# h2's columns by VectorE block transposition and a DRAM scratch instead of TensorE transposes

## The chip, the cores and the metric

The kernel runs on one core of a Trainium2 chip. The metric is device time in microseconds of one execution; 520.26 us is the median of three runs before the change. Engines: TensorE (PE), VectorE (DVE), ScalarE (ACT), GpSimd (POOL), and SyncE (SP), which issues most DMA transfers.

## The reference

The input x (16, 128, 64, 2) is a batch of complex weights; `h` is the real part of a state-space kernel table. Then come two residual layers on rows of length 1024, each behind a layernorm.

```python
K = einsum('chn,hnl->chl', Wc, exp(P)); h = K.real           # (16, 128, 1024)
h = h + einsum('bsk,nk->bsn', layernorm(h), weight * block_mask)
y = layernorm(h)
base = y @ W_base.T + b_base
weights = sparsemax(y @ W_router.T + b_router)               # 8 experts
h = h + base + einsum('bser,bse,ero->bso', y @ lora_A, weights, lora_B)
```

## The kernel before

The 2048 rows are cut into 16 tiles of 128 rows (16 batches by 8 heads). Before a loop, the weights are masked, centred and transposed and every fp32 operand is split into a high and a low part; a product is then three products (high by high, high by low, low by high). For each tile t:

- **Table.** `phases`, `exponentials`, `sines`, `v_factors`, `decay_b`, `table_v` and `table_b` build two small tables; `k_transposed` (PE, L439, sixteen matrix instructions) multiplies them, which gives the tile's columns in PSUM `turnp`. `k_high` (ACT, L717) and `k_low` (DVE, L1193) split them into `x1_hi` and `x1_lo`. `k_turn` (DVE, L1199) transposes 32 by 32 blocks of the same columns; SyncE writes them to a DRAM scratch `rows_out` in four pieces (L319) and reads them back as rows `h1` (L322).
- **First layer.** `attention` (PE, L455 on `acc_a`) multiplies; `k_sum` and `k_deviation` (ACT) with `h1_reciprocal` (DVE, L1204 to L1211) give the layernorm's factor; `attention_residual` (DVE, L1217) gives `h2`.
- **Second layer.** `h2_centre` and `h2_deviation` (ACT) centre h2 in place and take its deviation. `h2_transposes` (PE, L448) turns h2 into columns in `turnp`; `h2_high` (ACT, L752) and `h2_low` (DVE, L1246) split them. `lora_router` (L479, L481) and `base` (L455 on `acc_b`) multiply, `gates` (DVE, L1229 to L1240) forms the experts' weights, `gated_transpose`, `gated_high` and `gated_low` prepare them and `experts` multiplies. GpSimd's `add_bias` puts the mean back (L982) and adds the bias (L985); `result` (DVE, L1259) forms the output, which SyncE stores.

Each engine has its program written out by hand: a list of calls before the loop, then `step(t)`, run for tiles 2 to 11 in a loop of two steps a round and for 12 to 15 written out. Order across engines is by semaphores. A step on TensorE is: transposes of h2 of tile t-1, attention of t, table products of t+1, then lora_router, base and experts of t-1. `sines(t)` waits for `b_ready` of the tile before, since it overwrites factors that `table_b` reads.

## Time and profile before

| what | value |
|---|---|
| median of three runs | 520.26 us (519.95 to 521.26) |
| the profiled execution | 520.99 us, span 519.2 us |
| PE busy | 480.4 us (93%) |
| DVE busy | 408.4 us (79%) |
| ACT busy | 261.4 us (50%) |
| POOL busy | 125.7 us (24%) |

The span runs from the first to the last instruction of the profile; the execution's time has some 1.8 us more around it. Busy times of different engines overlap. Two operations of an engine can overlap by some 0.1 us at their borders, so that the time from one start to the next is what an operation costs its engine. Rows that name an idle time name the releaser behind an arrow.

### The profile page before, as it was taken

The page shows a single profiled execution, that of the slowest core. Times are in us where ns is not written, and L with a number is a line of the kernel's source. Part 1 is how long each engine was busy: PE and PEld are TensorE (multiplying, and loading weights), DVE is VectorE, ACT ScalarE, POOL GpSimd, SP SyncE. Part 2 cuts the span into 40 slices and gives each one's busy share as a digit, 9 for nine tenths or more (in the row PEclk, how much of TensorE's full clock was granted, in tenths as well). Part 3 has the DMA queues.
Part 4 walks back from the last instruction along what each step waited for, and adds up shares of the span by engine and source line. Part 5 has one row for each costly group of instructions (what it writes and reads, how often), then busy time and mean ns, then how long its engine had stood idle before and what let it go on. Part 6 is the DMA issues. An engine that isn't in the chain of part 4 may idle for free.

```text
span 519.2 us, 7441 instructions
## 1 busy us (share of the span) xinstructions
PE 480.4 (93%) x2467; PEld 406.1 (78%) x2467; DVE 408.4 (79%) x862; ACT 261.4 (50%) x476; POOL 125.7 (24%) x110
## 2 busy tenths in 40 slices
PE   1378789999999999999999999999999999999995
PEld 0267667877888888888888888888888888888884
DVE  7998979898988888888888888888888888854241
ACT  2848887576464626364554646362636455232200
POOL 0765597440303021020303030302102030303020
PEclk9998989999999999999999999999999999999999
DMA  8993113040403031212212030403121211313011
GB/s 286 391 338 51 63 42 122 1 127 6 126 3 110 16 88 38 81 45 68 59 40 86 10 116 0 109 17 88 38 81 47 67 56 26 96 31 92 1 40 40
DMA packets 28764, 40.83 MB, mean 79 GB/s; under 512 B 10760, under 2 KB 21192, under 8 KB 28744
## 3 DMA queue, kind: packets, MB, share of 16 engines
q1 hardware_dynamic: 28368, 40.49, 25.8%
q8 instruction: 10, 0.16, 0.1%
q10 hardware_dynamic: 376, 0.10, 0.1%
q14 instruction: 10, 0.08, 0.1%
HBM read 23.80 MB, written 16.78 MB: 78 GB/s over the span
## 4 chain that ended last, share of the span: by engine, by line
PE 90%; DVE 4%; issue 2%; ACT 2%; DMA 1%; POOL 1%; SPq 0%; DVEq 0%; POOLq 0%; ACTq 0%
PE acc_b L455 38%; PE acc_a L455 34%; PE turnp L439 6%; PE small L479 4%; PE turnp L448 3%; PE small L481 2%; PE acc_b L420 1%; PE acc_b L399 1%; DMA mask_raw<-in_L_attn_mask 1%; PE xps L429 1%; ACT wa_hi L668 1%; DVE mask_sum L1071 0%; DVE wa_raw L1080 0%; DVE wa_lo L1087 0%; PE small L487 0%
## 5 line engine op out<-in xcount | busy, mean ns | idle before, releaser
L982 POOL TENSOR_TENSOR h<-h,st 128x1024 f32<-128x1024 f32 x16 | 30.4, 1897 | 325.1 <-PE turnp L448 321.5
L455 PE MATMUL acc_a<-wa_hi,x_hi 128*128 128x512 f32 x256 | 83.2, 401 | 1.9 <-DVE wa_lo L1087 1.9
L455 PE MATMUL acc_b<-wb_hi,x_hi 128*128 128x512 f32 x256 | 83.9, 404 | 0.0
L455 PE MATMUL acc_a<-wa_hi,x_lo 128*128 128x512 f32 x256 | 81.3, 394 | 0.0
L455 PE MATMUL acc_a<-wa_lo,x_hi 128*128 128x512 f32 x256 | 81.2, 393 | 0.0
L455 PE MATMUL acc_b<-wb_lo,x_hi 128*128 128x512 f32 x256 | 80.5, 390 | 0.0
L455 PE MATMUL acc_b<-wb_hi,x_lo 128*128 128x512 f32 x256 | 80.5, 390 | 0.0
L455 PEld LDWEIGHTS acc_a<-wa_hi,x_lo 128*128 128x128 f32 x256 | 48.6, 190 | 10.4
L752 ACT ACTIVATE x_hi<-turnp 128x1024 fp32r<-128x1024 f32 x16 | 16.4, 1024 | 79.4 <-PE turnp L448 79.4
L455 PEld LDWEIGHTS acc_a<-wa_lo,x_hi 128*128 128x128 f32 x256 | 48.5, 189 | 10.0
L455 PEld LDWEIGHTS acc_b<-wb_hi,x_lo 128*128 128x128 f32 x256 | 48.1, 188 | 10.4
L455 PEld LDWEIGHTS acc_b<-wb_lo,x_hi 128*128 128x128 f32 x256 | 48.1, 188 | 10.4
L455 PEld LDWEIGHTS acc_a<-wa_hi,x_hi 128*128 128x128 f32 x256 | 47.3, 190 | 10.6 <-issue 2.0
L455 PEld LDWEIGHTS acc_b<-wb_hi,x_hi 128*128 128x128 f32 x256 | 44.8, 188 | 8.2
L1259 DVE SCALAR_TENSOR_TENSOR h<-acc_b,st,h 128x1024 f32<-128x1024 f32 (+1 forms) x17 | 20.7, 1221 | 25.5 <-PE acc_b L455 25.5
L985 POOL TENSOR_TENSOR h<-h,bias 128x1024 f32<-128x1024 f32 x16 | 39.5, 2467 | 1.3
L1193 DVE TENSOR_TENSOR x_lo<-turnp,x_hi 128x1024 fp32r<-128x1024 f32 x16 | 19.6, 1224 | 21.9 <-ACT x_hi L717 21.9
L439 PEld LDWEIGHTS turnp<-v_sb,b_sb 128*128 128x128 f32 x256 | 32.5, 200 | 3.6 <-issue 2.6
L439 PE MATMUL turnp<-v_sb,b_sb 128*128 128x128 f32 x256 | 32.9, 284 | 2.1 <-issue 2.1
L758 ACT ACTIVATE hw_hi<-small 128x128 fp32r<-128x128 f32 x16 | 4.4, 278 | 59.4 <-PE small L487 59.4
L479 PE MATMUL small<-wr,x_hi 128*128 128x272 f32 x128 | 32.2, 338 | 0.0
L692 ACT ACTIVATE er_t<-er_t 128x256 f32<-128x256 f32 x15 | 6.3, 419 | 48.9 <-DVE er_t L1112 48.9
(200 smaller groups left out, 937.0 us busy)
## 6 DMA issues: line engine op xcount, KB each, us to landing
h<-rows_out SPq DMA_DIRECT2D x16, 512.0 KB, 3.3
out<-h SPq DMA_DIRECT2D x15, 512.0 KB
rows_out<-b_sb SPq DMA_DIRECT2D x56, 128.0 KB, 2.3
mask_raw<-in_L_attn_mask SPq DMA_DIRECT2D x8, 512.0 KB, 9.9
wa_raw<-in_L_attn_weight SPq DMA_DIRECT2D x8, 512.0 KB, 10.5
wb_raw<-in_L_ffn_W_base SPq DMA_DIRECT2D x8, 512.0 KB, 6.7
rows_out<-tmp SPq DMA_DIRECT2D x8, 128.0 KB, 2.3
xn<-in_x SPq DMA_DIRECT2D x15, 64.0 KB
```

The costliest lines, as they stand in the source:

```text
L399: mm = pe.transpose(half_bank(i)[:, k * P:(k + 1) * P], every_eighth, ident)
L439: mm = pe.matmul(kt_pairs[:, h // HG, :, h % HG * C:(h % HG + 1) * C], b_sb[:, h, :, :].rearrange("p x y -> p (x y)"), v_sb[:, h, :, :], s ...
L448: mm = pe.transpose(turnp[:, k * P:(k + 1) * P], h2[par][:, k * P:(k + 1) * P], ident)
L455: return pe.matmul(cols, a, rows, start=first, stop=last)
L479: pe.matmul(small[:, 0:2 * CAT], x_hi[:, k, :], wr[:, k, :, :].rearrange("p s n -> p (s n)"), start=k == 0, stop=False)
L481: mm = pe.matmul(small[:, 0:CAT], x_lo[:, k, :], wr[:, k, 0, :], start=False, stop=k == KC - 1)
L692: act.activation(er_of(t), er_of(t), ACT.Exp).then_inc(tab_exp, 1)
L752: act.activation(x2_of(t)[0][:, :, :].rearrange("p k n -> p (k n)"), turnp[:, :], ACT.Copy)\
L982: pool.tensor_tensor(h2[par][:, :], h2[par][:, :], st2[:, par, 1:2].to_broadcast([P, L]), ALU.subtract)\
L985: pool.tensor_tensor(h2[par][:, :], h2[par][:, :], bias[:, :], ALU.add).then_inc(bias_added, 1)
L1193: dve.tensor_tensor(by_pair(lo), kt_pairs, by_pair(hi).bitcast(F), ALU.subtract).then_inc(kt_lo, 1)
L1259: dve.scalar_tensor_tensor(h, acc_b[:, cols], st2[:, par, 4:5], h, ALU.mult, ALU.add).then_inc(out_ready, 1)
```

## The change

In tiles 1 to 14 h2 doesn't go through TensorE. `h2_turn` (DVE) transposes 32 by 32 blocks of the centred h2 into `tmp`; `h2_columns` (SP) writes them to a DRAM scratch `cols_out` in four pieces and reads them back as columns into a buffer of their own, `x2_raw`; `h2_high` and `h2_low` split from there. Tiles 0 and 15 keep the transposes. ScalarE's `mean_add` puts the mean back, and GpSimd adds only the bias. `tmp` is now h2's, so `table_v` uses `turnp` for its second product, and `k_sum` and `k_deviation` write their unused output over `tmp` (`junk_tmp`). On VectorE `decay_b` moves out of `table_b`, `phases` to the start of a step. The orders before the loop are new on TensorE, ScalarE and VectorE; TensorE gets 14 products there (`keep_clock`) whose result nothing reads.

```diff
+        cols_out = nc.dram_tensor("cols_out", (4, 32, 4, KC * 32), F, kind="Internal").ap()
...
+        def by_dma(t):
+
+            return later(t, 1) and not at(t, TILES - 1)
+
+        def by_block(b):
+
+            return b[:, :, :].rearrange("p k (q r) -> p q k r", q=4)
+
+        x2_raw_block = x2_raw[:, :].rearrange("p (q k r) -> p q k r", q=4, k=KC)
...
+            def h2_columns(t):
+
+                sp.wait_ge(h2_turned, t)
+                for q in range(4):
+                    sp.dma_start(cols_out[:, :, q, :].rearrange("x i e -> i x e"),
+                                 tmp[q * 32:(q + 1) * 32, :].rearrange("i (x e) -> i x e", x=4)).then_inc(h2_out, 16)
+                sp.wait_ge(h2_out, t * 64)
+                sp.wait_ge(h2t_lo, t)
+                sp.dma_start(x2_raw[:, :], cols_out.rearrange("x i q e -> (x i) (q e)")).then_inc(h2_in, 16)
...
+                if by_dma(t):
+                    h2_columns(t)
...
+            def keep_clock(bank, n):
+
+                for _ in range(n):
+                    pe.matmul(bank, ident, kst[:, 0:2 * P], start=True, stop=True)
...
-                pe.wait_ge(kt_turned, t + 1)
-                h2_transposes(t - 1, 1 - par)
...
+            def mean_add(t, par):
+
+                if by_dma(t):
+                    act.wait_ge(h2_turned, t)
+                else:
+                    act.wait_ge(h2t_ready, 1 if at(t, 0) else 2)
+                act.wait_ge(h2_mean, t + 1)
+                mean = st2[:, par, 0:1]
+                act.activation(mean, mean, ACT.Copy, scale=1.0 / L).then_inc(mean_scaled, 1)
+                act.wait_ge(mean_scaled, t + 1)
+                act.wait_ge(h2_dev, t + 1)
+                act.activation(h2[par][:, :], h2[par][:, :], ACT.Identity, bias=mean).then_inc(mean_added, 1)
...
+                if later(t, 2):
+                    act.wait_ge(h2_out, t * 64 - 64)
+                act.activation(k_junk(t), h1[:, :], ACT.Copy, accum_out=st1[:, 0:1]).then_inc(h1_summed, 1)
 
...
-                act.wait_ge(h2t_ready, t + 1)
-                act.activation(x2_of(t)[0][:, :, :].rearrange("p k n -> p (k n)"), turnp[:, :], ACT.Copy)\
-                    .then_inc(h2t_hi, 1)
+                if by_dma(t):
+                    act.wait_ge(h2_in, t * 16)
+                    act.wait_ge(ffn_ready, t)
+                else:
+                    act.wait_ge(h2t_ready, 1 if at(t, 0) else 2)
+                hi = x2_of(t)[0]
+                if by_dma(t):
+                    act.activation(by_block(hi), x2_raw_block, ACT.Copy).then_inc(h2t_hi, 1)
+                else:
+                    act.activation(hi[:, :, :].rearrange("p k n -> p (k n)"), turnp[:, :], ACT.Copy).then_inc(h2t_hi, 1)
...
-                act.wait_ge(ffn_ready, t - 1)
-                h2_high(t - 1)
                 k_sum(t)
                 k_deviation(t)
+                h2_high(t - 1)
+                mean_add(t - 1, 1 - par)
                 if real(t + 2):
                     x_rows_twice(t + 2)
-                    exp_and_sin(t + 2)
+                    exponentials(t + 2)
+                    sines(t + 2)
...
-                pool.wait_ge(h2t_ready, t + 1)
-                pool.wait_ge(h2_dev, t + 1)
-                pool.tensor_tensor(h2[par][:, :], h2[par][:, :], st2[:, par, 1:2].to_broadcast([P, L]), ALU.subtract)\
-                    .then_inc(mean_added, 1)
...
-                second = v_second if not later(t, 2) else tmp[:, :].rearrange("p (h a c) -> p h a c", h=HT, a=NA)
+                second = v_second
...
-                decay_b(t)
                 dve.wait_ge(h1_in, t * 16)
+                dve.wait_ge(h2_out, t * 64 - 128)
+                dve.wait_ge(h1_dev, t)
...
+            def h2_turn(t, par):
+
+                dve.wait_ge(h2_dev, t + 1)
+                if at(t, 1):
+                    dve.wait_ge(h1_in, 32)
+                dve.transpose(tmp[:, :].rearrange("p (x k r) -> p k x r", x=4, k=KC), h2[par][:, :]).then_inc(h2_turned, 1)
...
-                dve.tensor_tensor(s[:, 4:5], s[:, 5:6], s[:, 7:8], ALU.mult).then_inc(s_chain, 1)
+                dve.tensor_scalar(s[:, 4:5], s[:, 5:6], s[:, 7:8], None, ALU.mult).then_inc(s_chain, 1)
...
-                dve.tensor_tensor(lo[:, :, :].rearrange("p k n -> p (k n)"), turnp[:, :],
-                                  hi[:, :, :].bitcast(F).rearrange("p k n -> p (k n)"), ALU.subtract)\
-                    .then_inc(h2t_lo, 1)
+                if by_dma(t):
+                    dve.tensor_tensor(by_block(lo), x2_raw_block, by_block(hi).bitcast(F), ALU.subtract).then_inc(h2t_lo, 1)
+                else:
+                    dve.tensor_tensor(lo[:, :, :].rearrange("p k n -> p (k n)"), turnp[:, :],
+                                      hi[:, :, :].bitcast(F).rearrange("p k n -> p (k n)"), ALU.subtract)\
+                        .then_inc(h2t_lo, 1)
...
+                if real(t + 2):
+                    phases(t + 2)
                 h2_low(t - 1)
-                h2_reciprocal(t - 1, 1 - par)
                 if real(t + 1):
                     table_b(t + 1)
                 h1_reciprocal(t)
-                if real(t + 2):
-                    phases(t + 2)
+                h2_reciprocal(t - 1, 1 - par)
                 dve.wait_ge(out_stored[par], t * 8 - 8 * par)
                 attention_residual(t, par)
+                if real(t + 2):
+                    v_factors(t + 2)
+                    decay_b(t + 2)
                 if real(t + 1):
                     k_low(t + 1)
+                    k_turn(t + 1)
                 gates(t - 1, 1 - par)
-                if real(t + 1):
-                    k_turn(t + 1)
-                if real(t + 2):
-                    v_factors(t + 2)
+                if by_dma(t):
+                    h2_turn(t, par)
                 gated_low(t - 1)
...
+            k_turn(2)
             k_low(2)
+            h2_turn(1, 1)
+            v_factors(3)
             gated_low(0)
```

TensorE at a step's border, before: the last products of `experts`, h2's transposes, and the first attention products.

```order
L455 MATMUL acc_b<-lb_hi,hw_hi 128x512
L455 MATMUL acc_b<-lb_lo,hw_hi 128x512 x2
L455 MATMUL acc_b<-lb_hi,hw_lo 128x512 x2
L448 MATMUL turnp<-kst,h_0 128x128 [waits h2_centred,kt_turned]
L448 MATMUL turnp<-kst,h_0 128x128 x7
L455 MATMUL acc_a<-wa_hi,x_hi 128x512 [waits kt_lo]
L455 MATMUL acc_a<-wa_hi,x_hi 128x512
L455 MATMUL acc_a<-wa_lo,x_hi 128x512 x2
```

The same border after the change (here L492 is the product helper):

```order
L492 MATMUL acc_b<-lb_hi,hw_hi 128x512
L492 MATMUL acc_b<-lb_lo,hw_hi 128x512 x2
L492 MATMUL acc_b<-lb_hi,hw_lo 128x512 x2
L492 MATMUL acc_a<-wa_hi,x_hi 128x512 [waits kt_lo]
L492 MATMUL acc_a<-wa_hi,x_hi 128x512
L492 MATMUL acc_a<-wa_lo,x_hi 128x512 x2
L492 MATMUL acc_a<-wa_hi,x_lo 128x512 x2
```

The eight transposes and their waits for `h2_centred` and `kt_turned` are gone; attention's own wait for `kt_lo` is left.

ScalarE across a step's border, before: `gated_high`, `h2_high` (L752), then `k_sum` and `k_deviation`.

```order
L758 ACTIVATE hw_hi<-small 128x128 [waits hwt_ready]
L752 ACTIVATE x_hi<-turnp 128x1024 [waits h2t_ready,ffn_ready]
L738 REGISTER_ALU [waits h1_in]
L739 ACTIVATE junk,st<-h 128x1024 [waits rs1_chain]
L743 ACTIVATE st<-st 128x1 [waits h1_summed]
L744 ISA
L745 ACTIVATE junk,st<-h,st 128x1024 [waits h1_stat]
L746 REGISTER_ALU
L747 ACTIVATE st<-st,kst 128x1 [waits h1_stat]
```

And after: `h2_high` is L819 and the first operation of `mean_add` L785.

```order
L826 ACTIVATE hw_hi<-small 128x128 [waits hwt_ready]
L797 REGISTER_ALU [waits h1_in]
L799 ISA [waits rs1_chain]
L800 ACTIVATE junk_tmp,st<-h 128x1024 [waits h2_out]
L804 ACTIVATE st<-st 128x1 [waits h1_summed]
L805 ISA
L806 ACTIVATE junk_tmp,st<-h,st 128x1024 [waits h1_stat]
L807 REGISTER_ALU
L808 ACTIVATE st<-st,kst 128x1 [waits h1_stat]
L813 REGISTER_ALU
L819 ACTIVATE x_hi<-x_raw 128x4x8x32 [waits ffn_ready,h2_in]
L785 ACTIVATE st<-st 128x1 [waits h2_mean,h2_turned]
```

`h2_high` moved behind `k_sum` and `k_deviation`, reads `x2_raw`, and waits for the scratch's read (`h2_in`); `k_sum` waits for the scratch's writes (`h2_out`).

VectorE at a step's end, before: `gated_low`, `table_v` (L1164 to L1167), `result` (L1259), and then the next step's `h2_low` (L1246).

```order
L1253 TENSOR_TENSOR hw_lo<-small,hw_hi 128x128 [waits hwt_hi]
L1163 REGISTER_ALU [waits b_ready,kt_ready,w_ready]
L1164 TENSOR_TENSOR v_sb<-xps,u 128x1024 [waits v_chain]
L1165 TENSOR_TENSOR tmp<-xps,u 128x1024
L1166 REGISTER_ALU
L1167 TENSOR_TENSOR v_sb<-tmp,v_sb 128x1024 [waits v_chain]
L1259 SCALAR_TENSOR_TENSOR h_1<-acc_b,st,h_1 128x1024 [waits bias_added,ffn_ready]
L1246 TENSOR_TENSOR x_lo<-turnp,x_hi 128x1024 [waits h2t_hi]
L1204 TENSOR_SCALAR st<-st 128x1 [waits h2_dev]
```

And after, from the last operation of `gates` (L1316) on: L1268 is `h2_turn`, L1231 to L1234 `table_v`, L1338 `result`.

```order
L1316 TENSOR_TENSOR hw_sb<-cat,gs 128x128 [waits gate_chain]
L1268 STREAM_TRANSPOSE tmp<-h_0 128x8x4x32 [waits h2_dev]
L1332 TENSOR_TENSOR hw_lo<-small,hw_hi 128x128 [waits hwt_hi]
L1230 REGISTER_ALU [waits b_ready,kt_turned,kt_ready,w_ready]
L1231 TENSOR_TENSOR v_sb<-xps,u 128x1024 [waits v_chain]
L1232 TENSOR_TENSOR turnp<-xps,u 128x1024
L1233 REGISTER_ALU
L1234 TENSOR_TENSOR v_sb<-turnp,v_sb 128x1024 [waits v_chain]
L1338 SCALAR_TENSOR_TENSOR h_1<-acc_b,st,h_1 128x1024 [waits bias_added,ffn_ready]
```

`h2_turn` stands between `gates` and `gated_low`, and `table_v` writes `turnp` where it wrote `tmp`.

## Rows read from the trace of the kernel before

**Rows 1.** Page, part 4: shares of the span on the chain that ended last.

```profile
PE 90%; DVE 4%; issue 2%; ACT 2%; DMA 1%; POOL 1%; SPq 0%; DVEq 0%; POOLq 0%; ACTq 0%
```

**Rows 2.** Chain in order of time, two loop steps (start us, us, what).

```profile
219.02 0.87 PE turnp L448 x8
219.89 10.92 PE acc_a L455 x48
230.81 1.78 PE turnp L439 x16
...
247.15 0.87 PE turnp L448 x8
...
472.83 10.93 PE acc_a L455 x48
```

**Rows 3.** Busy time by stretch (us), engine by engine, clock, DMA, GB/s.

```profile
27.80:104.83 77.03, 66.04 (x355) 55.99 (x354) 68.21 (x121) 56.13 (x102) 48.72 (x45) 0.96 0.33 96
190.88:219.02 28.14, 28.14 (x148) 23.89 (x146) 23.34 (x49) 14.29 (x26) 4.29 (x2) 1.00 0.20 58
```

**Rows 4.** VectorE, one loop step (start us, us, what, idle before).

```profile
222.87 1.49 DVE L1211 TENSOR_TENSOR st<-st 128x1 f32<-128x1 f32 x1
...
224.94 1.23 DVE L1183 TENSOR_TENSOR b_sb<-pp,qq 128x1024 f32<-128x1024 f32 x1
...
228.48 0.15 DVE L1204 TENSOR_SCALAR st<-st 128x1 f32<-128x1 f32 x1
...
229.23 0.16 DVE L1211 TENSOR_TENSOR st<-st 128x1 f32<-128x1 f32 x1
229.35 0.42 DVE L1112 TENSOR_TENSOR er_t<-dec,mul 128x256 f32<-128x256 f32 x1
...
231.74 1.28 DVE L1217 SCALAR_TENSOR_TENSOR h<-acc_a,st,h 128x1024 f32<-128x1024 f32 x1
...
234.73 1.23 DVE L1193 TENSOR_TENSOR x_lo<-turnp,x_hi 128x1024 fp32r<-128x1024 f32 x1 [1.70 <-ACT x_hi L717]
235.87 0.29 DVE L1229 COPY cat<-small 128x136 f32<-128x136 f32 x1
...
238.63 2.12 DVE L1199 STREAM_TRANSPOSE b_sb<-turnp 128x1024 f32<-128x1024 f32 x1
240.59 0.27 DVE L1137 TENSOR_TENSOR xy<-xy,er_t 128x128 f32<-128x128 f32 x1
```

**Rows 5.** SyncE's queue, one loop step (start us, us, what).

```profile
240.77 1.76 SPq L319 DMA_DIRECT2D rows_out<-b_sb  x4
244.37 0.34 SPq L322 DMA_DIRECT2D h<-rows_out  x1
```

**Rows 6.** Line L322, the read of the scratch: issue to landing.

```profile
DMA to landing us min/median/max: 3.2/3.3/4.1
```

**Rows 7.** ScalarE, one loop step (start us, us, what, idle before).

```profile
219.93 1.03 ACT L752 ACTIVATE x_hi<-turnp 128x1024 fp32r<-128x1024 f32 x1 [6.07 <-PE turnp L448]
...
230.25 1.28 ACT L700 ACT_TABLE_LOAD   x1
231.86 0.35 ACT L700 ACTIVATE xy<-gh_t,kst 128x64 f32<-128x64 f32 x1 [0.32 <-DVE a_t L1123]
...
233.31 0.48 ACT L705 ACTIVATE qq<-gh_t,kst 128x128 f32<-128x128 f32 x1
```

**Rows 8.** VectorE before the loop (start us, us, what).

```profile
81.03 0.28 DVE L1174 TENSOR_TENSOR pp<-pp,er_t 128x128 f32<-128x128 f32 x1
...
81.56 0.29 DVE L1137 TENSOR_TENSOR xy<-xy,er_t 128x128 f32<-128x128 f32 x1
...
82.69 1.22 DVE L1246 TENSOR_TENSOR x_lo<-turnp,x_hi 128x1024 fp32r<-128x1024 f32 x1
83.83 1.22 DVE L1164 TENSOR_TENSOR v_sb<-xps,u 128x1024 f32<-128x1024 f32 x1
```

**Rows 9.** GpSimd, the same loop step.

```profile
221.95 2.40 POOL L985 TENSOR_TENSOR h<-h,bias 128x1024 f32<-128x1024 f32 x1
```

More of the change, by code:

```diff
@@ L123, in build_vit_tower @@
         b_sb = sb("b_sb", [P, HT, NB1, NB0])
+        with nc.sbuf_tensor("junk_tmp", [P, L], BF) as junk_tmp:
+            pass
         tmp = sb("tmp", [P, L])
@@ L126, in build_vit_tower @@
         x1_raw, x1_lo = sb_twice("x1_raw", [P, L], F, "x1_lo", [P, KC, P])
-        x2_hi, x2_lo = sb("x2_hi", [P, KC, P], FR), sb("x2_lo", [P, KC, P], FR)
+        x2_hi = sb("x2_hi", [P, KC, P], FR)
+        x2_lo = sb("x2_lo", [P, KC, P], FR)
+        with nc.sbuf_tensor("junk", [P, L], BF) as junk:
+            pass
+        x2_raw = sb("x2_raw", [P, L])
         h1 = sb("h1", [P, L])
         h2 = [sb(f"h2_{i}", [P, L]) for i in range(2)]
-        junk = sb("junk", [P, L], BF)
         hw_sb = sb("hw_sb", [P, E, R])
@@ L591, in _ @@
             attention(1, 1)
-            attention(1, 2)
             wb_half(10)
@@ L596, in _ @@
             h2_transposes(0, 0)
+            attention(1, 2)
             wb_half(12)
@@ L608, in _ @@
             lora_router(0)
-            k_transposed(2)
+            x_transposes(3)
+            attention(1, 7)
             pe.wait_ge(wb_high, 2 * NWT)
@@ L813, in _ @@
             wa_highs(13)
-            q_tanh(1)
+            k_sum(0)
             wa_highs(14)
             wa_highs(15)
+            k_deviation(0)
             wb_highs(0)
+            wb_highs(1)
+            q_sines(1)
             x_rows_twice(2)
-            wb_highs(1)
+            k_high(1)
+            sines(2)
+            wb_highs(2)
+            exponentials(2)
+            wb_highs(3)
+            wb_highs(4)
+            h2_centre(0, 0)
+            wb_highs(5)
+            wb_highs(6)
+            h2_deviation(0, 0)
+            wb_highs(7)
+            wb_highs(8)
+            wb_highs(9)
+            wb_highs(10)
+            wb_highs(11)
+            wb_highs(12)
             act.wait_ge(lora_in, 16 * KC)
@@ L822, in _ @@
             act.activation(wr[:, :, 0, :], cat_raw, ACT.Copy).then_inc(cat_hi, 1)
-            k_sum(0)
-            k_deviation(0)
-            q_sines(1)
-            wb_highs(2)
-            wb_highs(3)
-            k_high(1)
-            wb_highs(4)
-            wb_highs(5)
-            exponentials(2)
-            wb_highs(6)
-            wb_highs(7)
-            sines(2)
-            wb_highs(8)
-            wb_highs(9)
-            h2_centre(0, 0)
-            wb_highs(10)
-            wb_highs(11)
-            wb_highs(12)
             wb_highs(13)
+            h2_high(0)
             x_rows_twice(3)
-            h2_high(0)
-            h2_deviation(0, 0)
+            k_sum(1)
             wb_highs(14)
             wb_highs(15)
-            k_sum(1)
+            mean_add(0, 0)
             k_deviation(1)
             h2_centre(1, 1)
+            k_high(2)
+            sines(3)
             act.wait_ge(lorb_in, 16)
             act.activation(lb_hi[:, :], lb_raw[:, :], ACT.Copy).then_inc(lorb_hi, 1)
-            k_high(2)
+            h2_deviation(1, 1)
+            gated_high(0)
             exponentials(3)
-            gated_high(0)
-            sines(3)
-            h2_deviation(1, 1)
             steps(act, step)
@@ L861, in _ @@
             h2_high(TILES - 1)
+            mean_add(TILES - 1, 1)
             gated_high(TILES - 1)
@@ L1308, in _ @@
             wa_mask(1)
-            reciprocal_of_norm(0)
+            wa_mask(2)
+            v_factors(0)
+            wa_lows(0)
+            wa_mask(3)
+            wa_lows(1)
+            decay_b(0)
             mask_sums(4)
-            wa_mask(2)
-            wa_mask(3)
+            table_v(0)
+            mask_sums(5)
             wa_mask(4)
-            decay_b(0)
-            v_factors(0)
-            mask_sums(5)
-            wa_lows(0)
-            wa_lows(1)
-            table_v(0)
+            wa_lows(4)
             mask_sums(6)
-            wa_lows(4)
+            phases(1)
             wa_lows(5)
+            wa_mask(5)
+            q_arguments(1)
             mask_sums(7)
-            wa_mask(5)
-            phases(1)
             k_low(0)
-            wa_mask(6)
+            k_turn(0)
             wa_lows(8)
             wa_lows(9)
-            q_arguments(1)
+            wa_mask(6)
             wa_mask(7)
+            router_columns()
             decay_b(1)
-            k_turn(0)
+            reciprocal_of_tanh(1)
             wa_lows(12)
@@ L1353, in _ @@
             wb_lows(6)
+            k_turn(1)
             wb_lows(7)
-            k_turn(1)
             wb_lows(8)
+            decay_b(2)
             wb_lows(9)
@@ L1360, in _ @@
             wb_lows(11)
+            v_factors(2)
             wb_lows(12)
             wb_lows(13)
-            decay_b(2)
-            v_factors(2)
             h2_low(0)
@@ L1368, in _ @@
             wb_lows(15)
-            phases(3)
-            h2_reciprocal(0, 0)
             h1_reciprocal(1)
@@ L1373, in _ @@
             attention_residual(1, 1)
+            phases(3)
+            h2_reciprocal(0, 0)
             dve.wait_ge(biasr_in, 16)
             gates(0, 0)
+            k_turn(2)
             k_low(2)
+            h2_turn(1, 1)
+            v_factors(3)
             gated_low(0)
-            k_turn(2)
-            v_factors(3)
+            decay_b(3)
+            table_v(3)
             dve.wait_ge(ffn_ready, 1)
             result(0, 0)
-            table_v(3)
             steps(dve, step)
```

108 lines of the change are left out of this document (60 added, 48 removed).

## The prediction

> **What bounds the kernel now.** I read the chain that ended last first: 90% of it is TensorE [rows 1]. Then the same chain in order of time, over the loop [rows 2]: eight transposes of h2 (0.87 us), 48 attention products (10.92), the table products (1.78), and so on to the next transposes at 247.15. No piece of another engine stands between them, so a step lasts 247.15 - 219.02 = 28.13 us and the loop is TensorE without a gap; from 219.89 to 472.83 nine steps average 28.10. The reader is to see in the busy times by stretch (second row of [rows 3]) that the next engine, VectorE, does 23.3 us of that step and that the clock is full (1.00, the 2.4 GHz level). Before the loop it is otherwise: from 27.8 to 104.8 us TensorE is busy 66.0 of 77.0 us and VectorE 68.2 (first row of [rows 3]); there nobody binds alone.
>
> **The change part by part.** *Removed:* the eight transposes of each step whose h2 goes by DMA. In the loop that is 0.87 us of TensorE [rows 2], so TensorE alone would need 28.13 - 0.87 = 27.26. From the attention products of tile 3 to those of tile 15 there are twelve such steps, all of which the change touches; the most to be had there is 12 x (28.10 - 27.26) = 10.1 us. The last tile keeps its transposes, so the tail gives nothing.
>
> *Added:* the columns must now make a round trip, and what counts is when the round trip, started by one step's h2_turn, lets the next step's h2_turn start. I sum it from the end of h2_turn.
>
> The scratch. k_turn does the same journey today: it ends at 238.63 + 2.12 = 240.75 [rows 4], its four writes are issued at 240.77 and the read at 244.37 [rows 5], 3.62 us after; the read lands 3.3 us after issue in the median [rows 6]. Sizes and row lengths of h2's four writes and one read are the same, so 6.92. SyncE is free for it: k_turn stands a gates block and a transposition ahead of h2_turn, 2.76 plus over 1 us, against the 3.62 + 0.34 that its own sequence takes [rows 4, 5]; nearly even, so at worst some tenths. Behind the read waits only the store of the tile before.
>
> ScalarE. h2_high is 1.03 [rows 7]; with two handovers of 0.02 (240.75 to 240.77) the sum is 7.99. k_sum and k_deviation stand ahead of it, but wait only for the writes, not the read, so I cost them nothing; their cover is the 3.3 us read. mean_add comes behind h2_high, and with it, one small and one full-width operation later, GpSimd's bias addition starts.
>
> VectorE. h2_low: 1.14 (82.69 to 83.83) [rows 8]. table_b without its decay: 3.54 (224.94 to 228.48) [rows 4]. Sum 12.67. VectorE is not late for h2_low: gated_low, table_v, result and phases need about 7.3 us of the 8.
>
> GpSimd. The bias addition takes 2.40 [rows 9]. Today it meets one small VectorE operation with both inputs in SBUF: L1211 takes 1.49 there and 0.16 six us later [rows 4], and its end, 224.36, is the end of GpSimd's 2.40 (224.35). After the change the addition falls beside h2_low and table_b. Nothing here shows it beside those, so the bounds are 0 and 2.40; I take 2.40, since L1211 stood still until the whole addition was done: 15.07 at b_ready. The Trainium skill (SBUF — State Buffer, "Who interferes with whom") says that a VectorE instruction with two SBUF inputs blocks fully against a GpSimd one that reads SBUF, and h2_low, which read PSUM, becomes such a one; by that rule the cost is 2.40 and speaks against the change, by the 0.16 of an undisturbed operation it would be nothing and the sum 2.40 shorter.
>
> ScalarE again: the sines wait for b_ready with their table load in front, which today is early. Load 1.28, the six sines 1.93 (231.86 to 233.31 + 0.48) [rows 7]: 18.28. The stretch of h1's and h2's reciprocals and the residual lies beside that (0.87 + 0.87 + 1.28 = 3.0) [rows 4].
>
> VectorE to the next h2_turn: decay_b 0.53, v_factors 1.13 [rows 8], k_low 1.14, k_turn 1.96, gates 2.76 [rows 4]: 7.52, sum 25.80.
>
> h2_turn itself. The only transposition shown takes 2.12 for 1024 columns; every other operation of that width takes 1.2 [rows 4]. k_turn writes with a step of eight values; h2_turn reads SBUF straight through and writes runs of 32. Bounds 1.2 and 2.12; since its access is that of the plain operations, I take 1.22. The Trainium skill (Vector Engine (DVE) Microarchitecture Reference, 3.8 "The reshape front-end and per-opcode configuration") has the transposing array at one element per cycle per lane; the 2.12 of k_turn doesn't agree with it as it stands, and no run here shows whether the write step is why. By the rule the round trip is 27.0, by the row 27.9.
>
> The round trip is thus 27.02 us, against TensorE's 27.26. Two cycles that close, with a read that lands between 3.2 and 4.1 [rows 6], don't run at the longer one exactly: I take 27.4 for a step, where TensorE waits a tenth or two at the table products. Twelve steps: 12 x (28.10 - 27.4) = 8.4.
>
> VectorE's own load: 23.34 busy, less 1.33 for L1211 (now a one-input form that need not stand still), plus 1.22 and at most 2.40, is 25.6; it stays below 27.26, by less than before.
>
> *Moved:* the orders before the loop. TensorE idles 77.0 - 66.0 = 11.0 us there and VectorE 8.8 [rows 3]. The new order does k_turn(0) some 2 us earlier against VectorE's other work, and fills TensorE's pauses with 14 products that keep it active (its granted clock is 0.96 there); against that, gated_low(0) now stands behind h2_turn(1) and v_factors(3), so the first experts can wait, and the first scratch trip starts only there. I bound this by a loss of 3 and a gain of 6, and take a gain of 1.5, a fifth of what VectorE idles.
>
> Sum: the profiled execution took 520.99 (span 519.2); less 8.4 and 1.5 is 511.1. The median shown is 520.26, 0.73 below the profiled one, so 510.4. About 0.3% (1.6 us) is what a measurement here can tell from no change.
>
> **Rivals.** *The transposition costs 2.12.* For: the only row of its kind. Against: the write step. The round trip is then 27.92, with the same tenth or two 28.05, no better than today's 28.10: 12 x 0.05 + 1.5 leaves 518.2, on the edge of no change. TensorE would simply wait for b_ready instead of transposing.
>
> *The scratch trip is longer than k_turn's (slower).* Its writes follow the read of h1, and its read runs up against the store of the tile before; both are 512 KB. Each us beyond 6.92 prolongs each of twelve steps once the 0.24 of slack is gone; from 8.0 on the kernel is slower by the loop. With landings at the 4.1 shown as the longest, for writes (2.3 now) and read alike, the trip is 6.92 + 1.8 + 0.8 = 9.5; halfway, 8.2, a step is 28.3 and with half the prologue's gain lost the time is 520.3 + 2.4 - 0.8 = 522; at 9.5 it is 29.6, 520.3 + 18 - 0.8 = 538. Against: in the loop the median lies 0.1 above the shortest.
>
> *The cover holds better.* GpSimd finds no gap until table_b is through; then the sum is 24.6, steps are TensorE's 27.26, and with an order before the loop that gains 4 the time is 520.3 - 10.1 - 4 = 506.
>
> **How the numbers follow.** Forecast case (steps of 27.3 to 27.6; 507 to 514): 0.50. Transposition dear (518): 0.20. Longer trip (522 to 538): 0.12. Better cover (506): 0.18. Range: 504 (a full 10.1 and the bound of 6 before the loop) to 520.5 (the dear transposition without any gain before the loop); that leaves out the longer trip and little else. Faster by over 0.3% (below 518.7): 0.50 + 0.18 + 0.12 of the dear transposition's 0.20 = 0.80; within 0.3%: the other 0.08; slower 0.12.
>
> **What would show it.** In the profile after: h2's transposes gone from the chain but for two tiles; a step of 27.3 to 27.6; x2_raw landing about 6.9 us after h2_turn's end; h2_turn at 1.2 or 2.1; one of h2_low and table_b's operations at 3.6 instead of 1.2, ending with GpSimd's addition; TensorE's only wait in a step at the table products for b_ready. Wrong would be a step above 28, or a wait at lora_router, which would say that h2_low, not table_b, is late.

## The result, and the profile after

The changed kernel takes 539.12 us (median of 4 runs, 536.75 to 540.3), the kernel before 520.47 on the same chip: a ratio of 1.0351, 95% interval 1.0309 to 1.0393. It is slower by 18.7 us where 10 were forecast as a gain, 28.7 off the predicted 510.4 and outside the range.

The profiled execution took 538.15 us (span 536.3). The chain that ended last, by engine, against 90% TensorE before [rows 1]:

```profile
DVE 28%; DMA 20%; ACT 15%; PE 14%; SPq 13%; issue 8%; DVEq 1%; ACTq 0%
```

The chain is no longer one engine; it is a round trip through VectorE, SyncE, the DMA engines and ScalarE. The same chain in order of time over two steps, its pieces of 0.8 us and more, from the landing of the first writes to the next table (start us, us, what). L368 writes h2's columns to the scratch and L372 reads them back, L819 is h2_high, L1251 to L1254 are table_b, L742 the load of the sines' table, L1261 k_low, L1275 k_turn, L800 k_sum:

```profile
251.90 3.13 DMA cols_out<-tmp
255.05 3.22 DMA x_raw<-cols_out
258.29 1.07 ACT x_hi L819
259.71 0.82 issue
260.53 1.22 DVE b_sb L1251
261.75 3.36 DVE tmp L1252
265.13 1.24 DVE b_sb L1254
266.44 1.28 ACT L742
271.53 1.14 DVE x_lo L1261
272.67 2.15 DVE b_sb L1275
276.15 2.36 DMA rows_out<-b_sb
278.53 3.73 DMA h<-rows_out
282.43 1.28 ACT L800
283.72 1.16 ACT junk_tmp L800 x2
...
290.12 1.22 DVE b_sb L1251
...
318.62 1.22 DVE b_sb L1251
```

Where TensorE alone stood in [rows 2], there is none of it in these two steps. Table_b starts at 260.53, 290.12, 318.62: steps of 29.59 and 28.50 in turn, against 28.13. The alternation has two chains: one step goes through the columns' trip, the next through h1's read and ScalarE. Busy times by stretch, answering to [rows 3]; the second row is two steps:

```profile
27.80:104.83 77.03, 66.02 (x369) 54.97 (x369) 66.13 (x131) 58.28 (x109) 44.90 (x43) 0.98 0.35 101
250.20:308.20 58.00, 55.93 (x275) 45.93 (x274) 50.94 (x102) 33.83 (x58) 6.62 (x2) 1.00 0.31 93
```

TensorE pauses 2.07 us in two steps at full clock, and VectorE has 7 us to spare: neither binds alone. SyncE's queue in those two steps, answering to [rows 5] (L338 writes k_turn's result, L341 reads h1):

```profile
246.39 1.76 SPq L338 DMA_DIRECT2D rows_out<-b_sb  x4
250.08 0.34 SPq L341 DMA_DIRECT2D h<-rows_out  x1
250.54 1.88 SPq L368 DMA_DIRECT2D cols_out<-tmp  x4
255.05 0.34 SPq L372 DMA_DIRECT2D x_raw<-cols_out  x1
...
278.53 0.34 SPq L341 DMA_DIRECT2D h<-rows_out  x1
278.98 1.99 SPq L368 DMA_DIRECT2D cols_out<-tmp  x4
283.70 0.34 SPq L372 DMA_DIRECT2D x_raw<-cols_out  x1
```

The columns' first write is issued 0.46 us after h1's read, each time. From there to the scratch's read passes 4.51 and 4.72 us; for k_turn's result, in the kernel before, it was 3.60 (240.77 to 244.37). The read itself lands 3.2 us after issue in the median, as [rows 6] would have it. VectorE from h2_low (L1323) to h2_turn (L1268), and GpSimd's addition, answering to [rows 4, 9]:

```profile
259.39 1.22 DVE L1323 TENSOR_TENSOR x_lo<-x_raw,x_hi 128x1024 fp32r<-128x1024 f32 x1 [0.76 <-ACT x_hi L819]
260.53 1.22 DVE L1251 TENSOR_TENSOR b_sb<-pp,qq 128x1024 f32<-128x1024 f32 x1
261.67 3.43 DVE L1252 TENSOR_TENSOR tmp<-pp,qq 128x1024 f32<-128x1024 f32 x1
265.13 1.23 DVE L1254 TENSOR_TENSOR b_sb<-b_sb,tmp 128x1024 f32<-128x1024 f32 x1
...
277.40 1.24 DVE L1268 STREAM_TRANSPOSE tmp<-h 128x1024 f32<-128x1024 f32 x1
```

```profile
260.71 3.30 POOL L1052 TENSOR_TENSOR h<-h,bias 128x1024 f32<-128x1024 f32 x1 [25.10 <-ACT h L788]
```

L1252 takes 3.43 us instead of 1.22 and ends 1.1 after GpSimd's 264.01: it stood still until the addition was done. GpSimd's took 3.30 instead of 2.40, its first 0.9 to 1.0 beside L1251. The transposition h2_turn is 1.24. Last, ScalarE in the second of the two steps, against [rows 7]:

```profile
282.43 1.28 ACT L800 ACT_TABLE_LOAD   x1 [4.24 <-DMA h<-rows_out]
283.72 1.06 ACT L800 ACTIVATE junk_tmp<-h 128x1024 bf16<-128x1024 f32 x1
...
286.40 1.28 ACT L808 ACT_TABLE_LOAD   x1
287.70 0.29 ACT L808 ACTIVATE st<-st,kst 128x1 f32<-128x1 f32 x1
287.90 1.04 ACT L819 ACTIVATE x_hi<-x_raw 128x1024 fp32r<-128x1024 f32 x1
```

Two loads of a function table, in the first step of each loop round alone. ScalarE enters the loop with the table of the exponentials, but comes back to its top with that of the roots, so the loads stand at the top for both; k1_sqrt below bears that out. In the step before, k_sum starts with the writes' landing (255.06) and h2_high at 258.29, 3.24 after the read's issue; here it is 4.20. The first of the two loads ends when the writes land (283.71) and costs nothing; the second prolongs the trip.

### The profile page after: what moved, and what is told of

Read it like the earlier page. It is cut to its first block, busy times and chain, and to the rows that moved or that the text cites. A ratio compares the mean times of both kernels' runs of the same rounds, so it can differ in the third digit from the quotient of the medians.

```text
span 536.3 us, 7446 instructions
## 1 busy us (share of the span) xinstructions
PE 480.0 (89%) x2379; PEld 397.3 (74%) x2379; DVE 432.2 (81%) x876; ACT 293.3 (55%) x516; POOL 106.0 (20%) x94
## 4 chain that ended last, share of the span: by engine, by line
DVE 28%; DMA 20%; ACT 15%; PE 14%; SPq 13%; issue 8%; DVEq 1%; ACTq 0%
DVE tmp L1252 8%; PE acc_b L492 7%; DMA cols_out<-tmp 6%; DMA rows_out<-b_sb 6%; DVE b_sb L1275 5%; DMA x_raw<-cols_out 5%; PE acc_a L492 4%; DMA h<-rows_out 3%; SPq L352 3%; SPq L338 3%; DVE b_sb L1254 3%; DVE b_sb L1251 3%; ACT L742 3%; ACT x_hi L819 2%; DVE x_lo L1261 2%
## 5 line engine op out<-in xcount | busy, mean ns | idle before, releaser
L1052 POOL TENSOR_TENSOR h<-h,bias 128x1024 f32<-128x1024 f32 x16 | 50.2, 3139 | 365.2 <-ACT h L788 365.2
L492 PE MATMUL acc_b<-wb_hi,x_hi 128*128 128x512 f32 x256 | 84.3, 405 | 0.0
L492 PE MATMUL acc_a<-wa_hi,x_hi 128*128 128x512 f32 x256 | 82.7, 399 | 0.8 <-ACT wa_hi L710 0.8
L492 PE MATMUL acc_a<-wa_lo,x_hi 128*128 128x512 f32 x256 | 81.5, 395 | 0.0
L492 PE MATMUL acc_b<-wb_lo,x_hi 128*128 128x512 f32 x256 | 81.1, 393 | 0.0
L492 PE MATMUL acc_a<-wa_hi,x_lo 128*128 128x512 f32 x256 | 80.9, 392 | 0.0
L492 PE MATMUL acc_b<-wb_hi,x_lo 128*128 128x512 f32 x256 | 80.9, 392 | 0.0
L492 PEld LDWEIGHTS acc_a<-wa_hi,x_lo 128*128 128x128 f32 x256 | 48.3, 189 | 11.0
L492 PEld LDWEIGHTS acc_a<-wa_lo,x_hi 128*128 128x128 f32 x256 | 48.5, 189 | 10.5
L492 PEld LDWEIGHTS acc_b<-wb_hi,x_lo 128*128 128x128 f32 x256 | 48.1, 188 | 10.9
L492 PEld LDWEIGHTS acc_b<-wb_lo,x_hi 128*128 128x128 f32 x256 | 48.1, 188 | 10.7
L492 PEld LDWEIGHTS acc_a<-wa_hi,x_hi 128*128 128x128 f32 x256 | 48.0, 189 | 10.7 <-issue 1.0
L476 PE MATMUL turnp<-v_sb,b_sb 128*128 128x128 f32 x256 | 34.8, 293 | 20.1 <-issue 11.0
L476 PEld LDWEIGHTS turnp<-v_sb,b_sb 128*128 128x128 f32 x256 | 32.5, 205 | 25.7 <-issue 25.5
L492 PEld LDWEIGHTS acc_b<-wb_hi,x_hi 128*128 128x128 f32 x256 | 45.5, 191 | 7.3
L1252 DVE TENSOR_TENSOR tmp<-pp,qq 128x1024 f32<-128x1024 f32 x13 | 44.6, 3432 | 0.0
L800 ACT ACTIVATE junk_tmp<-h 128x1024 bf16<-128x1024 f32 x14 | 14.8, 1058 | 51.1 <-DMA cols_out<-tmp 51.0
L1338 DVE SCALAR_TENSOR_TENSOR h<-acc_b,st,h 128x1024 f32<-128x1024 f32 (+1 forms) x17 | 20.7, 1220 | 24.1 <-PE acc_b L492 24.1
L1323 DVE TENSOR_TENSOR x_lo<-x_raw,x_hi 128x1024 fp32r<-128x1024 f32 x14 | 17.2, 1225 | 24.7 <-ACT x_hi L819 24.7
```

The costliest lines, as they stand in the source:

```text
L476: mm = pe.matmul(kt_pairs[:, h // HG, :, h % HG * C:(h % HG + 1) * C], b_sb[:, h, :, :].rearrange("p x y -> p (x y)"), v_sb[:, h, :, :], s ...
L492: return pe.matmul(cols, a, rows, start=first, stop=last)
L1052: pool.tensor_tensor(h2[par][:, :], h2[par][:, :], bias[:, :], ALU.add).then_inc(bias_added, 1)
L1252: dve.tensor_tensor(b_terms(tmp), *b_factors(t, 1), ALU.mult).then_inc(b_chain, 2)
L1323: dve.tensor_tensor(by_block(lo), x2_raw_block, by_block(hi).bitcast(F), ALU.subtract).then_inc(h2t_lo, 1)
L1338: dve.scalar_tensor_tensor(h, acc_b[:, cols], st2[:, par, 4:5], h, ALU.mult, ALU.add).then_inc(out_ready, 1)
```

## The experiments

A step is the time from one tile's first attention product to the next one's; attention(3) and attention(15) are where it starts for these tiles. k4 and k8 leave out part or all of h1's read and k9 the reordering of k_turn's result in every second step, so these three are for timing alone. In the diffs `...` marks what is left out.

| kernel | median us | ratio to before, 95% interval | attention(3) | step | attention(15) |
|---|---|---|---|---|---|
| before | 520.06 to 520.54 | | 135.25 | 28.13 | 472.59 |
| after | 539.12 | 1.035 [1.031, 1.039] | 139.01 | 29.6 / 28.6 | 489.55 |
| k1_sqrt | 537.06 | 1.030 [1.027, 1.033] | 140.62 | 28.7 to 29.2 | 489.86 |
| k2_bias_late | 513.65 | 0.987 [0.984, 0.989] | 136.84 | 27.42 | 465.61 |
| k4_h1_quarter | 524.64 | 1.008 [1.006, 1.011] | 139.49 | 28.7 / 27.7 | 475.81 |
| k5_orders_alone | 527.50 | 1.013 [1.010, 1.015] | 138.91 | 28.31 | 478.55 |
| k8_no_h1_read | 519.48 | 0.998 [0.997, 1.000] | 139.67 | 27.4 to 27.6 | 471.13 |
| k9_plain_turn | 537.98 | 1.035 [1.033, 1.037] | 139.88 | 27.6 to 31.2 | 488.44 |
| k7_shift64 | 523.03 | 1.005 [1.004, 1.007] | 135.08 | 28.31 | 474.51 |
| k10_bias_late_aligned | 517.82 | 0.996 [0.995, 0.998] | 135.75 | 27.72 | 468.23 |
| k12_bias_late_placed | 510.27 | 0.982 [0.980, 0.983] | 135.29 | 27.23 | 461.75 |
| k14_up128 | 527.70 | 1.014 [1.013, 1.016] | 134.45 | 28.62 | 477.64 |
| k15_up256 | 520.46 | 1.000 [0.999, 1.001] | 134.90 | 28.13 | 472.24 |
| k16_all_up128 | 519.91 | 0.999 [0.998, 1.000] | 133.93 | 28.13 | 471.28 |
| k13_all | 509.20 | 0.980 [0.978, 0.982] | 134.43 | 27.23 | 460.90 |

The column of steps leaves out a few of the twelve at either end: 27.83 and 31.84 in the changed kernel, 27.96, 30.33, 31.59 and 28.05 in k1, 28.51 in k8.

**k1_sqrt**

```diff
             exponentials(3)
+            act.activation(wa_neg[:, 0:1], col(COL_HALF), ACT.Sqrt)
             steps(act, step)
```

> One Sqrt of a single column is added on ScalarE after exponentials(3), so that the loop is entered with the same function table as its back edge has, and the two table loads at the loop's top go. Theory A (the loop step is the round trip h2_turn - scratch - h2_high - table_b - sines - next h2_turn, and every microsecond on it counts): the first step of each loop round falls from 29.6 to about 28.4 us, five rounds, so 539.1 - 6 = about 533 us. Rival B (the scratch trip alone is late, ScalarE's loads lie beside it): steps still alternate 28.4 and 29.6, 539 us.

The loads went and so did the alternation, but the time fell by 2.1, not 6, and the runs of the two kernels overlap (534.94 to 538.52 against 536.75 to 540.3). In the eight steps from 164 to 366 us the trip from h2_turn's end to h2_high is 8.3 to 8.8 us, where the changed kernel has 8.1 to 8.3 and 9.2 to 9.35 in turn. From the read's issue to h2_high it is 3.3 in all of them instead of 4.2 in every second one, so ScalarE no longer outlasts the read. But from the first write's issue to the read's it is 4.90 instead of 4.74, and the 3.3 is 3.32 where the changed kernel's steps without loads have 3.21. So the loads did prolong every second step, as A has it, and part of what they cost came back in the transfers; why those became longer is open. What the loads are worth in the whole time is not shown by this run.

**k2_bias_late**

```diff
             def add_bias(t, par):
+                if real(t + 2):
+                    pool.wait_ge(b_ready, t + 3)
                 pool.wait_ge(mean_added, t + 1)
```

> GpSimd's addition of the bias waits until table_b is through, so it no longer stands beside table_b on VectorE. Theory A: L1252's operation falls from 3.43 to 1.22 us and each of 12 steps with it by about 2.2, unless TensorE's 27.26 or a later wait comes first: steps of 27.3 to 27.6, about 516 to 521 us. Rival B (the scratch trip sets the step whatever stands behind it on VectorE, since the trip's start would be moved too, or the addition meets another operation on the path instead): less than 0.5 per step, 533 to 539 us.

Faster than expected: 25.5 us off the changed kernel, with trips as long as there (8.2 to 9.7). Of the 23.9 us that attention(15) comes sooner, 2.2 lie ahead of attention(3). Table_b's second operation (L1254 here) is back at 1.22, and GpSimd's addition at 2.4:

```profile
251.90 1.22 DVE L1253 TENSOR_TENSOR b_sb<-pp,qq 128x1024 f32<-128x1024 f32 x1
253.03 1.22 DVE L1254 TENSOR_TENSOR tmp<-pp,qq 128x1024 f32<-128x1024 f32 x1
```

```profile
255.67 2.40 POOL L1054 TENSOR_TENSOR h<-h,bias 128x1024 f32<-128x1024 f32 x1 [24.48 <-DVE b_sb L1256]
```

The steps are all TensorE's again: in its chain, the products of the experts run straight into the next tile's attention:

```profile
213.75 5.51 PE acc_b L492 x24
219.26 10.99 PE acc_a L492 x48
230.25 1.78 PE turnp L476 x16
...
246.67 10.99 PE acc_a L492 x48
```

247.15 - 219.02 is now 246.67 - 219.26 = 27.41. Taking 2.2 us out of steps of 29.6 and 28.5 leaves 27.4 and 26.3, both within it. Rival B falls: the trip sets the step only together with what stands behind it. But TensorE itself needs 27.42, not the 27.26 of the prediction, 10.99 us for 48 products instead of 10.93; k7 follows that up.

**k4_h1_quarter**

```diff
-                sp.dma_start(h1[:, :], rows_out.rearrange("g r l -> (g r) l")).then_inc(h1_in, 16)
+                if later(t, 2):
+                    sp.dma_start(h1[0:32, :], rows_out[0]).then_inc(h1_in, 16)
...
```

> From the third tile on only a quarter of h1 (128 KB of 512) is read back from its scratch; three quarters of h1 keep the values of an earlier tile. Theory A with contention (the writes of h2's columns land late because h1's read was issued 0.4 us ahead of them): the writes land about 2.3 us after issue instead of 3.1 to 3.4, the trip falls from 8.07 to about 7.0 us, a step by 1.1, and the time to about 525 us; the steps that wait for h1 at the loop's top gain too. Rival C (the writes are late by themselves, 2.3 was never theirs): trip 8.0 as before, 536 to 539 us.

As A expected (524.64 against 525). Page, the DMA issues, in the changed kernel and then in this one (KB each, median us from issue to landing):

```profile
cols_out<-tmp SPq DMA_DIRECT2D x56, 128.0 KB, 3.4
```

```profile
cols_out<-tmp SPq DMA_DIRECT2D x56, 128.0 KB, 2.4
```

The same 128 KB writes land 1.0 us sooner when h1's read ahead of them is a quarter; the read of the scratch stays (3.3 instead of 3.2). From the first write's issue to the scratch's read it is 3.79 to 3.85 in eleven steps. The trip is 7.2 to 7.7 us, and 8.3 in the steps with ScalarE's loads. The Trainium skill (SBUF — State Buffer, "Can I just issue two DMAs to hit both halves?") says that all DMAs of a kernel share the same 16 engines and largely serialize; at the 358 GB/s that the summary of that page gives for transfers between HBM and SBUF, the 384 KB left out are an estimated 1.1 us. The 1.0 measured agrees with it.

**k5_orders_alone** (the last columns through TensorE as before; new orders kept)

```diff
         def by_dma(t):
 
-            return later(t, 1) and not at(t, TILES - 1)
+            return False
...
             def step(t, par):
+                pe.wait_ge(kt_turned, t + 1)
+                if real(t + 1):
+                    pe.wait_ge(v_ready, t + 2)
+                h2_transposes(t - 1, 1 - par)
                 pe.wait_ge(kt_lo, t + 1)
...
```

> All of h2's columns go by TensorE again; the new orders and the mean on ScalarE stay. Theory A (the round trip makes the loop slow): steps go back to TensorE's 28.1 us, and with the earlier start of the loop's work (some 4 us before the loop) the time is 515 to 521 us. Rival D (the new orders themselves, or GpSimd's addition beside table_b, cost the time): 528 us or more, with steps above 28.5.

527.5: neither fits. The loop is TensorE's without a gap, as A says, but at 28.31 instead of 28.13 (2.2 us in twelve steps; k7 below has the same 28.31), and attention(3) starts at 138.91, 3.7 later than before. So the new orders had no gain before the loop to give this kernel, though in the changed kernel the residual of the second tile starts at 89.8 us instead of 94.2. Its added wait for v_ready, which the kernel before doesn't have at that place, is part of this start, so the 3.7 isn't the orders' alone.

**k8_no_h1_read** (with k1's Sqrt besides)

```diff
+                if later(t, 3):
+                    sp.dma_start(h1[0:N, 0:2], lam).then_inc(h1_in, 16)
+                    return
                 sp.wait_ge(k_out, (t + 1) * 16 * Q)
...
             exponentials(3)
+            act.activation(wa_neg[:, 0:1], col(COL_HALF), ACT.Sqrt)
...
                 dve.wait_ge(h2_out, t * 64 - 128)
+                dve.wait_ge(k_out, t * 16 * Q)
                 dve.wait_ge(h1_dev, t)
```

> From the fourth tile on the read of h1 is left out (h1 keeps old values; a read of a few bytes stands in its place, and SyncE doesn't wait for the rows before it issues the columns' writes); the Sqrt of k1_sqrt is in. GpSimd's addition still stands beside table_b. Theory A' (the predicted sum was right but for the scratch trip; measured in the changed kernel, what follows the trip takes 20.3 us, and the trip is long by h1's read, SyncE's order and ScalarE's two table loads): the trip falls from 8.2 to 9.3 to about 6.9 to 7.2 us, a step to 27.4 to 27.6, so the time to 539.1 - 12 x 1.7 = about 519 us (the loss before the loop stays). Rival (what follows the trip is long as well, or the trip is long by itself): steps of 28 us or more, 526 us or more.

519.48 against 519. The trip is 6.8 to 7.2 us in eleven steps, the prediction's 6.92, and the step 27.4 to 27.6, its 27.4, with GpSimd's block still in table_b (in most steps 3.31 at its third operation instead of its second). One trip, from h2_turn's end (245.28) by the first write, the scratch's read and h2_high, and TensorE's chain beside it:

```profile
244.04 1.24 DVE L1273 STREAM_TRANSPOSE tmp<-h 128x1024 f32<-128x1024 f32 x1
245.30 1.75 SPq L371 DMA_DIRECT2D cols_out<-tmp  x4
248.98 0.34 SPq L375 DMA_DIRECT2D x_raw<-cols_out  x1
252.36 1.06 ACT L822 ACTIVATE x_hi<-x_raw 128x1024 fp32r<-128x1024 f32 x1 [0.38 <-DMA x_raw<-cols_out]
...
250.01 10.99 PE acc_a L495 x48
```

This is the run that names the failed step: with the trip as long as the prediction had it, the loop no longer waits for the round trip. From 140 to 415 us its chain is TensorE's alone, which needs 27.42 at these addresses (k2). So the step of 27.4 doesn't confirm the other terms of the sum; those are measured in the changed kernel.

**k9_plain_turn**

```diff
...
+                elif par == 0:
+                    dve.transpose(turned_of(t), turnp[:, :]).then_inc(kt_turned, 1)
...
```

> In every second step of the loop k_turn writes its result straight through instead of with a step of eight values (h1 is then wrong in those steps); in the other steps it is as it was. Theory W (the write step, not the transposition, makes k_turn 2.2 us): the straight ones take 1.24 us, as h2_turn does, the others 2.2, and the loop gains about 1 us in every second step, some 5 to 6 us in all: 533 us. Rival P (the read from PSUM makes it 2.2): all stay at 2.2, 539 us.

W holds for the operation. Duration in ns, min/median/max, of k_turn written straight (L1278) and with the step (L1280):

```profile
L1278 DVE STREAM_TRANSPOSE b_sb<-turnp x7: 1239/1240/1240, 126.9 to 476.4; 128x1024 f32<-128x1024 f32 x7
L1280 DVE STREAM_TRANSPOSE b_sb<-turnp x6: 2195/2220/2233, 156.9 to 447.4; 128x1024 f32<-128x1024 f32 x6
```

Both read the same PSUM, so PSUM isn't it. The Trainium skill (SBUF — State Buffer, "Door 1: The DMA port swizzle") says that an access that goes on to another 16-byte line of SBUF pays for it; a step of eight values does so each time, and 2.22 against 1.24 agrees. For the time, the expectation fell: 1.1 us less instead of 5 to 6, which the spread of the runs doesn't tell from nothing. In several of these steps table_b ended 9.3 to 9.8 us after h2_high's start instead of 8.1, with GpSimd's block at its first operation; that wasn't followed further.

**k7_shift64**

```diff
-        gt, neg_gt, flip = sb("gt", [P, 1]), sb("neg_gt", [P, 1]), sb("flip", [P, 1])
+        signs_sb = sb("signs_sb", [P, 3])
+        gt, neg_gt, flip = (signs_sb[:, i:i + 1] for i in range(3))
```

> The kernel before, with its three one-value columns gt, neg_gt and flip laid into one buffer of three, as in the changed kernel; that moves every later SBUF buffer, x1 and x2 among them, down by 64 bytes and changes nothing else. Theory L (TensorE's products took 10.99 us for 48 instead of 10.93, and a step 27.42 instead of 27.26, because x1 and x2 lie 64 bytes off): a step of 28.3 us instead of 28.13, about 522.5 us. Rival (the new orders or the other engines' accesses slow the products): 28.13, 520.5 us.

Theory L: 523.03. The kernel before, with nothing but later buffers 64 bytes lower, has the slower products:

```profile
220.24 11.00 PE acc_a L456 x48
```

**k10_bias_late_aligned** (k2 with this besides)

```diff
-        dt_k, dt_r, dt_p, dt_w = (sb(n, [P, 2]) for n in ("dt_k", "dt_r", "dt_p", "dt_w"))
+        dt_sb, dt_w = sb("dt_sb", [P, 6]), sb("dt_w", [P, 2])
+        dt_k, dt_r, dt_p = (dt_sb[:, 2 * i:2 * i + 2] for i in range(3))
```

> k2_bias_late with three small buffers merged as well, so that x1, x2 and all else behind them lie 64 bytes lower still, at a multiple of 128 bytes as in the kernel before. Theory L: 48 products at 10.93 us, a step of 27.26 instead of 27.42, 513.65 - 12 x 0.16 - about 0.5 = 511.3 us. Rival: 10.99 and 513.6 us as without.

Both fall: slower than k2, 517.82, 48 products at 11.15 to 11.16 and steps of 27.72. A multiple of 128 bytes isn't what helps; at 128 bytes off the products are worse than at 64.

**k12_bias_late_placed** (k2 with this besides)

```diff
-        signs_sb = sb("signs_sb", [P, 3])
-        gt, neg_gt, flip = (signs_sb[:, i:i + 1] for i in range(3))
+        signs_sb = sb("signs_sb", [P, 24])
+        gt, neg_gt, flip, tau = (signs_sb[:, i:i + 1] for i in range(4))
+        wa_sum = signs_sb[:, 8:8 + NWT]
...
```

> k2_bias_late with the buffers from xn on laid 64 bytes higher (the one buffer of three columns takes 96 bytes, and tau and wa_sum lie in it), so that v, b, tmp, x1 and x2 have the addresses of the kernel before. Theory L' (the products' rate goes with these addresses: 10.93 us for 48 there, 11.00 at 64 bytes less, 11.16 at 128 less): 10.93 again, a step of 27.26, which is the figure that the prediction had for TensorE alone; 513.65 - 12 x 0.16 - 0.5 = about 511.2 us. Rival (something else of these kernels slows the products by 0.6%): 11.0 and 513.6.

L' holds: 510.27 and a step of 27.23, with the products no slower than in the kernel before:

```profile
217.15 10.88 PE acc_a L493 x48
```

**k14_up128, k15_up256, k16_all_up128** (the kernel before with 128 or 256 bytes left free ahead of xn; or 128 ahead of every buffer, the weights' too; the diff is k14's)

```diff
+        sb("pad", [P, 32])
         xn = sb("xn", [P, N, 2])
```

> The kernel before with 128 bytes left free ahead of xn, so that everything behind lies 128 bytes higher. Theory L1 (the rate falls with each step down and goes on rising upward): 48 products in under 10.93 us, a step below 28.1, 517 to 520 us. Theory L2 (the equal offset of x1, x2 and of the weights' buffers is the best there is): 11.0 to 11.2, 523 to 527 us.

> The same with 256 bytes left free. By L1 faster still or as with 128, by L2 slower than before: 523 to 528 us; if the pattern repeats within 256 bytes it is the time of the kernel before, 520.3 us.

> The kernel before with 128 bytes left free ahead of all its buffers, so that the weights' buffers lie 128 bytes higher as well as x1 and x2 (in k14_up128 x1, x2 alone moved, and 48 products took 11.15 to 11.19 us). Theory R (what counts is how x1 and x2, VectorE's and ScalarE's buffers lie against the weights' buffers): 10.93 us and 520.4. Theory M (what counts is the address itself, modulo 256): 11.16 us and 527.7.

Attention's 48 products in the three, in this order:

```profile
220.52 11.19 PE acc_a L456 x48
```

```profile
219.54 10.92 PE acc_a L456 x48
```

```profile
218.58 10.92 PE acc_a L456 x48
```

L2 holds (527.7, just above its range), with a pattern that repeats within 256 bytes, and R: moving the weights' buffers along brings the rate back. Which of the buffers that moved together has to lie so, x1 and x2 or those that VectorE and ScalarE use, is not shown.

**k13_all** (k12 with k1's Sqrt and SyncE's load of x moved)

```diff
             k_rows(2)
-            load_x(4)
...
             h2_columns(1)
+            load_x(4)
```

> k12_bias_late_placed with the Sqrt of k1_sqrt, so that the two table loads leave the loop's top and the first trip, and with SyncE's load of tile 4's x moved behind the first trip's read, so that the first writes of h2's columns don't stand behind it. In the trace of k12 that load (0.62 us) is on the chain ahead of the first trip, and the table loads in it (1.0). Theory A (the loop is TensorE's, 27.23 a step, only the first trip is to be had): 510.3 - 1.6 = 508.7 us. Rival (something else before the loop is late in its place): 510.3.

509.2, the fastest, 2.0% below the kernel before. The first trip fell from 11.05 us in k12 to 10.0 and attention(3) came 0.9 sooner; A's 1.6 was a little too much. The runs of the two overlap (509.56 to 512.07 and 508.97 to 511.17), so of the 1.1 between the medians only these 0.9 in the traces are shown.

## Why the prediction was wrong

The round trip was the right model, and its sum failed above all in one term. The trace of the changed kernel over one step, from h2_turn's end (250.20) to the next (278.64), by the prediction's terms:

| term | predicted | measured |
|---|---|---|
| scratch trip, h2_turn's end to h2_high | 6.92 | 8.09; 9.26 in the next step; 8.77 mean of ten |
| h2_high, h2_low, table_b with GpSimd's block | 8.15 | 8.07 |
| sines to h2_turn's end | 11.95 | 12.28 |
| sum | 27.02 | 28.44; next step 29.56 |

The third term is 0.33 over as well, in pieces of a tenth or less in and between its operations (k_turn costs 2.05 for 1.96). With the last two terms as measured, the predicted trip would give 27.27, so the 0.24 of slack against TensorE's 27.26 was never there.

- **The step that failed** is "Sizes and row lengths of h2's four writes and one read are the same, so 6.92. SyncE is free for it". The mean excess of 1.85 has three parts. The writes: about 1.1, since h1's read is issued 0.46 us ahead of them and k_turn's own writes had no such neighbour; k4 shows 1.0 of it. SyncE: 0.3, since the first write waits behind h1's read in its queue; the prediction called it "nearly even, so at worst some tenths", but of a margin of 0.24 that alone was too much. ScalarE: 1.0 in every second step, because "so I cost them nothing; their cover is the 3.3 us read" holds only without the two table loads; k1, without them, still has a mean trip of 8.55. In k8, without these, the trip is 7.0 and the loop TensorE's.
- **What it had as the rival.** The longer trip, with 28.3 us a step at 8.2 and 29.6 at 9.5, is what happened: 28.4 at 8.1 and 29.6 at 9.3. Its chance of 0.12 was too low: the prediction itself named h1's 512 KB read as the neighbour, and set it aside by landings in a trace where the two never met.
- **GpSimd's block** was right: 2.40 taken, 2.21 measured (3.43 - 1.22). The Trainium skill (SBUF — State Buffer, "Who interferes with whom") says that a VectorE instruction with two SBUF inputs contends with a GpSimd one that reads SBUF; the trace agrees. That the term was right doesn't make the block harmless: with the trip as it is, moving the addition behind table_b (k2) gives the loop back to TensorE. The prediction had this as better cover at 506; k12 measures 510.27, and 27.23 a step against its 27.26, without the 4 us before the loop. That 510.27 is nearly the forecast's 510.4 is luck: the forecast had slower steps of 27.4 and a gain of 1.5 before the loop.
- **h2_turn** was right: 1.24 against 1.22; the rival of 2.12 fell, and k9 shows why.
- **What lies before the loop** was wrong: a gain of 1.5 taken, a loss of 3.8 measured at attention(3) (139.01 against 135.25). In this trace the loss is not ahead of tile 2, whose attention starts at 105.32 against 105.67; it is in the step from there to tile 3, the one with the first trip, which lasts 33.69 instead of 29.58. In k1, k2, k4 and k8 tile 2 starts at 106.7 to 108.3, so a gain ahead of it is not shown either. The first trip lasts 11.4 us: its writes are issued 2.6 after h2_turn(1), behind k_rows(2) and a load of x, and ScalarE's two loads lie in it, of which the second prolongs it. With GpSimd's block gone (k2) the loss is 1.6, and with the addresses put right too (k12) nothing.
- **TensorE's own 27.26** held only at the old addresses; the change moved x1 and x2 by 64 bytes, 0.16 a step. The prediction didn't look for it. It lay below the round trip in the changed kernel's loop and cost nothing there, but it is most of the 3.4 between k2 and k12.

The miss between the profiled executions is 27.1 us (538.15 against 511.1): 5.3 of it before the loop (3.8 and the 1.5 that didn't come), and 21.7 in twelve steps of 29.21 on average instead of 27.4. The changed kernel's last step of these lasted 31.84, with writes that took 5.7 to 6.7; those also stand out in k1 and k2 at the same place. What delays them is open, but the trace shows a neighbour for them: one transfer of the instruction queue falls between 452 and 462 us and one between 480 and 490, and there is none from 150 to 400, most of the loop. The first of them (queue, kind: packets, MB, share of 16 engines):

```profile
q8 instruction: 1, 0.02, 0.6%
```

The slow writes of k1, k2, k9, k12 and k13 behind the loop each have one beside them too. No run takes such a transfer away, so this is a coincidence in time and not a shown cause.
